# Attention loop of a four-layer graph network: the target one-hot on GpSimd, targets loaded first, the MLP's first layer beside its second

## What is computed

```python
wk = relu(edge_features @ k_w1 + k_b1) @ k_w2 + k_b2      # an MLP of two layers
wv = relu(edge_features @ v_w1 + v_b1) @ v_w2 + v_b2
k  = wk * sum_s sh[:, s] * (x_dst @ Cqk[:, s, :])          # s over 9
v  = wv * sum_s sh[:, s] * (x_dst @ Cv[:, s, :])
attn  = sum over each head of q[edge_src] * k              # 8 heads of 16
amax  = segment_max(attn, edge_src)
ex    = exp(attn - amax[edge_src])
denom = segment_sum(ex, edge_src)
upd   = segment_sum(v * ex / denom[edge_src], edge_src)
```

## Time and profile before

| what | us |
|---|---|
| median of three runs | 5155.87 |
| lowest, highest | 5151.41, 5162.44 |
| the profiled execution, its own time | 5154.97 |
| its span, first to last instruction | 5153.2 |
| mean granted TensorE clock, of 1 | 0.854 |

### The profile page before, as it was taken

The page is one execution under the profiler, slowest core; times in us unless marked ns, Lnnn a source line. Parts: engine busy times, 40 slices in busy tenths (PEclk is TensorE's granted clock), DMA queues, the critical chain, the costliest instruction groups (busy, mean ns, idle before and its releaser), DMA issues. The chain is left out here.

```text
span 5153.2 us, 91855 instructions
## 1 busy us (share of the span) xinstructions
PE 4427.7 (86%) x21874; PEld 3147.8 (61%) x21874; DVE 4161.0 (81%) x9462; ACT 2259.1 (44%) x4914; POOL 2409.1 (47%) x2660
## 2 busy tenths in 40 slices
PE   1788877879999999999999999999998677777777
PEld 0222343557777777777777777777777566666665
DVE  5999956479999999999999999999996455555554
ACT  0777740045555555555555555555553100000000
POOL 1000000045555555555555555555552377777774
PEclk7999978789999999999999999999998555555555
DMA  2121116377777777777777777777773244444442
GB/s 56 75 92 83 75 50 262 122 170 175 176 176 175 177 176 175 174 176 175 176 174 174 175 175 176 174 175 176 174 175 78 63 102 103 103 103 102 103 102 64
DMA packets 576584, 719.34 MB, mean 140 GB/s; under 512 B 204519, under 2 KB 338727, under 8 KB 572583
## 3 DMA queue, kind: packets, MB, share of 16 engines
q1 hardware_dynamic: 517910, 634.65, 49.1%
q0 software_dynamic: 52288, 81.11, 7.3%
q10 hardware_dynamic: 6288, 2.48, 0.2%
HBM read 663.58 MB, written 54.36 MB: 139 GB/s over the span
## 5 line engine op out<-in xcount | busy, mean ns | idle before, releaser
L1328 POOL DMA_INDIRECT attn_rows<-x_twice,attn_idx x808 | 988.4, 1223 | 237.6 <-issue 198.3
L1684 POOL DMA_INDIRECT msg_rows<-a_rows,msg_idx x808 | 778.9, 964 | 370.3 <-issue 241.2
L1271 ACT CAST attn_z_hi<-attn_z 128x512 fp32r<-128x512 f32 x1010 | 621.9, 620 | 184.9 <-DVE attn_z L1526 155.1
L1526 DVE TENSOR_TENSOR attn_z<-attn_xt,attn_sh 128x512 f32<-128x512 f32 x1010 | 679.0, 689 | 27.1 <-ACT attn_xt L1259 6.1
L1347 POOL TENSOR_TENSOR acc_den<-acc_den,attn_sums 128x256 f32 x808 | 582.0, 720 | 188.7 <-POOL acc_den L1347 151.9
L1722 PE MATMUL msg_at_dst<-msg_bwin,msg_pick 128*128 128x64 f32 x1616 | 397.7, 428 | 270.8 <-DVE msg_pick L1748 193.3
L1722 PEld LDWEIGHTS msg_at_dst<-msg_bwin,msg_pick 128*128 128x128 f32 x1616 | 359.9, 328 | 351.1 <-DVE msg_pick L1748 227.9
L1532 DVE TENSOR_TENSOR attn_z_lo<-attn_z,attn_z_hi 128x512 fp32r<-128x512 f32 x808 | 551.2, 682 | 0.8 <-ACT attn_z_hi L1271 0.7
L1662 ACT ACTIVATE msg_msg<-msg_pre 128x256 f32<-128x256 f32 x202 | 84.1, 417 | 941.5 <-DVE msg_pre L1763 937.1
L1349 POOL MEMSET acc_den<- 128x6656 f32 x1 | 5.6, 5646 | 978.6 <-POOLq L90 978.6
L538 PE MATMUL count_bank<-count_key_hot,count_lo_hot 128*128 128x400 bf16 x1395 | 328.7, 346 | 137.8 <-DVE count_key_hot L496 134.5
(11 more groups left out here) (293 smaller groups left out, 10927.0 us busy)
## 6 DMA issues: line engine op xcount, KB each, us to landing
attn_sh<-in_edge_sh SPq DMA_DIRECT2D x404, 640.0 KB
attn_dst<-dst_scaled SPq DMA_DIRECT2D x202, 256.0 KB
attn_qwin<-q_rows SPq DMA_DIRECT2D x808, 64.0 KB
attn_mask<-dst_step SPq DMA_DIRECT2D x202, 256.0 KB, 3.4
msg_dst<-dst_scaled SPq DMA_DIRECT2D x202, 256.0 KB, 3.2
counts<-chunk SPq DMA_DIRECT2D x15, 3100.0 KB, 9.7
chunk_late<-counts SPq DMA_DIRECT2D x15, 3100.0 KB, 10.4
attn_feat<-in_edge_feat SPq DMA_DIRECT2D x404, 64.0 KB
```

The lines of the kernel that those rows point to most:

```text
L1271: nc.scalar.copy(z_hi[p][:, c, :], z[:, c % 2, :]).then_inc(high_sb, 1)
L1328: pool.indirect_dma_start(rows[p][:, t, :], None, dram["x_twice"], bass.IndirectOffsetOnAxis(ap=idx[p][:, t:t + 1], axis=0)).then_inc(rows ...
L1526: dve.tensor_tensor(z[:, c % 2, :], xt[p][:], sh[p][:, c, :], ALU.mult).then_inc(z_ready, 1)
L1684: pool.indirect_dma_start(rows[p][:, t, :], None, dram["a_rows"], bass.IndirectOffsetOnAxis(ap=idx[p][:, t:t + 1], axis=0)).then_inc(rows_ ...
```

## The change

- `make_onehot` leaves VectorE. GpSimd makes it now, for group g instead of g-1: after the backward scan of g (`topped`) it runs four `tensor_scalar` comparisons of 128 columns, each with one column of targets as scalar. Their four target columns are copied to a small tile `local[p]` by ScalarE first. `onehot` gets two buffers. GpSimd's loop is then add, make_onehot, gather.
- `pick` gets two buffers, and VectorE's `make_pick(g+2)` moves from behind `maxima(g)` to ahead of it, into the place of `make_onehot`.
- SyncE loads `dst` first of a group's transfers.
- The MLP's first layer leaves `prepare` and stands directly ahead of the second layer, behind the k product. Its second half goes to the bank `b_attn` instead of `b_v`. ScalarE's third rounding `high(g+1, 2)` goes ahead of the relus.

```diff
@@ scalar body @@
                 if next:
+                    high(g + 1, q, 2)
                     hidden(g + 1, q)
-                    high(g + 1, q, 2)
...
+                if front:
+                    if not (is_first(g, 0) or is_first(g, 1)):
+                        act.wait_ge(onehot_ready, g - 1)
+                    nc.scalar.copy(local[p][:], sb["dst_local"][:, bass.ds(TG * g, TG)]).then_inc(local_sb, 1)
@@ gpsimd @@
+            def make_onehot(g, p):
+
+                pool.wait_ge(topped, g + 1)
+                pool.wait_ge(local_sb, g + 1)
+                if not (is_first(g, 0) or is_first(g, 1)):
+                    pool.wait_ge(sum_ps, g - 1)
+                pool.sem_inc(pool_go, 1)
+                for t in range(TG):
+                    op = pool.tensor_scalar(onehot[p][:, t, :], sb["iota_row"][:],
+                                            local[p][:, t:t + 1], None, ALU.is_equal)
+                op.then_inc(onehot_ready, 1)
...
             with pool.Fori(0, G // 2 - 3) as n:
                 add(2 * n + 1, 1)
+                make_onehot(2 * n + 3, 1)
                 gather(2 * n + 6, n + 3, 0, False)
                 add(2 * n + 2, 0)
+                make_onehot(2 * n + 4, 0)
                 gather(2 * n + 7, n + 3, 1, False)
@@ sync load @@
+                if not first:
+                    sp.wait_ge(pick_ready, g - 1)
+                sp.dma_start(dst[p][:], dram["dst_scaled"][bass.ds(g * GE, GE)].partition_broadcast(P)
+                             ).then_inc(dst_in[p], 16)
                 if not first:
                     sp.wait_ge(hid_ps, g - 1)
...
-                    sp.wait_ge(pick_ready, g - 1)
-                sp.dma_start(dst[p][:], dram["dst_scaled"][bass.ds(g * GE, GE)].partition_broadcast(P)
-                             ).then_inc(dst_in[p], 16)
-                if not first:
                     sp.wait_ge(q_ps, g - 1)
@@ tensor @@
                 mm.then_inc(xt_ps, 1)
+
+            def hidden(g, n, p):
                 pe.wait_ge(feat_in[p], 32 * (n + 1))
                 if not is_first(g, 0):
                     pe.wait_ge(hid_sb, 2 * g)
                 if not (is_first(g, 0) or is_first(g, 1)):
-                    pe.wait_ge(vw_ready, g - 1)
+                    pe.wait_ge(shifted, 2 * (g - 1))
                 nc.tensor.matmul(b_hid_vt[:, 0:GE // 2], sb["L2_w1"][0:D, :], feat[p][0:D, :], start=True, stop=True)
-                nc.tensor.matmul(b_v[:, 0:GE // 2], sb["L2_w1"][D:P, :], feat[p][D:P, :], start=True,
+                nc.tensor.matmul(b_attn[:, 0:GE // 2], sb["L2_w1"][D:P, :], feat[p][D:P, :], start=True,
                                  stop=True).then_inc(hid_ps, 1)
...
                     split_product(b_k, "L2_Cqk", g, p, True).then_inc(k_ps, 1)
+                if next:
+                    hidden(*after(g, n, p))
+                if front:
                     pe.wait_ge(hid_sb, 2 * (g + 1))
...
-                    if next:
-                        pe.wait_ge(hid_sb, 2 * (g + 2))
                     split_product(b_v, "L2_Cv", g, p, False).then_inc(v_ps, 1)
...
+                    if next:
+                        pe.wait_ge(hid_sb, 2 * (g + 2) - 1)
                     for t in range(TG):
                         nc.tensor.transpose(b_hid_vt[:, t * P:(t + 1) * P], vx[:, t * P:(t + 1) * P], sb["ident"][:])
...
                     pe.wait_ge(u_ready, g + 1)
+                    if next:
+                        pe.wait_ge(hid_sb, 2 * (g + 2))
                     nc.tensor.matmul(b_attn[:], sb["head_sum"][:], u[:], start=True, stop=True).then_inc(attn_ps, 1)
@@ vector @@
             def make_pick(g, n, p):
                 dve.wait_ge(dst_in[p], 16 * (n + 1))
-                if not is_first(g, 0):
-                    dve.wait_ge(q_ps, g)
+                if not (is_first(g, 0) or is_first(g, 1)):
+                    dve.wait_ge(q_ps, g - 1)
...
                     dve.tensor_tensor(vw[p][:], b_v[:], wv[:], ALU.mult).then_inc(vw_ready, 1)
-                if back:
-                    make_onehot(g - 1)
+                if has_two(g):
+                    make_pick(*in_two(g, n, p))
                 if front:
                     maxima(g, n, p)
-                if has_two(g):
-                    make_pick(*in_two(g, n, p))
```

More of the change, by code:

```diff
@@ L1167, in attention_loop @@
                                 "kw_ready", "u_ready", "vw_ready", "dve_set"))
-        xt_sb, hid_sb, w_sb, ex_sb, vt_sb, sum_sb, high_sb = (
-            ph.sem(n) for n in ("xt_sb", "hid_sb", "w_sb", "ex_sb", "vt_sb", "sum_sb", "high_sb"))
+        xt_sb, hid_sb, w_sb, ex_sb, vt_sb, sum_sb, high_sb, local_sb = (
+            ph.sem(n) for n in ("xt_sb", "hid_sb", "w_sb", "ex_sb", "vt_sb", "sum_sb", "high_sb", "local_sb"))
         vx_ready = ph.sem("vx_ready")
@@ L1190, in attention_loop @@
         wv = ph.sb("wv", [P, GE])
-        pick = ph.sb("pick", [P, TG, P])
-        onehot = ph.sb("onehot", [P, TG, P])
+        pick = [ph.sb(f"pick{p}", [P, TG, P]) for p in two]
+        onehot = [ph.sb(f"onehot{p}", [P, TG, P]) for p in two]
         u = ph.sb("u", [P, GE])
@@ L1200, in attention_loop @@
         zero = ph.sb("zero", [P, 1])
+        local = [ph.sb(f"local{p}", [P, TG]) for p in two]
         vt = ph.sb("vt", [P, TG, HD])
@@ L1263, in hidden @@
                 act.wait_ge(hid_ps, g + 1)
-                for half, bank in enumerate((b_hid_vt, b_v)):
+                for half, bank in enumerate((b_hid_vt, b_attn)):
                     nc.scalar.activation(hid[p][:, half * (GE // 2):(half + 1) * (GE // 2)], bank[:, 0:GE // 2], ACT.Relu,
@@ L1355, in _ @@
             gather(3, 1, 1, False)
+            make_onehot(0, 0)
             gather(4, 2, 0, False)
+            make_onehot(1, 1)
             add(0, 0)
+            make_onehot(2, 0)
             gather(5, 2, 1, False)
@@ L1360, in _ @@
                 add(2 * n + 1, 1)
+                make_onehot(2 * n + 3, 1)
                 gather(2 * n + 6, n + 3, 0, False)
                 add(2 * n + 2, 0)
+                make_onehot(2 * n + 4, 0)
                 gather(2 * n + 7, n + 3, 1, False)
             add(G - 5, 1)
-            for g in range(G - 4, G):
-                add(g, g % 2)
+            for g in range(G - 3, G):
+                make_onehot(g, g % 2)
+                add(g - 1, (g - 1) % 2)
+            add(G - 1, 1)
         @block.sync
@@ L1424, in pick_q @@
                 for t in range(TG):
-                    mm = nc.tensor.matmul(b_q[:, t * P:(t + 1) * P], qwin[p][:, t, :], pick[:, t, :],
+                    mm = nc.tensor.matmul(b_q[:, t * P:(t + 1) * P], qwin[p][:, t, :], pick[p][:, t, :],
                                           start=True, stop=True)
@@ L1483, in body @@
                     for t in range(TG):
-                        nc.tensor.matmul(b_wk_sum[:, t * P:(t + 1) * P], vt[:, t, :], onehot[:, t, :],
+                        nc.tensor.matmul(b_wk_sum[:, t * P:(t + 1) * P], vt[:, t, :], onehot[q][:, t, :],
                                          start=True, stop=True)
                     for t in range(TG):
-                        mm = nc.tensor.matmul(b_wv_den[:, t * P:(t + 1) * P], et[:, t, :], onehot[:, t, :],
+                        mm = nc.tensor.matmul(b_wv_den[:, t * P:(t + 1) * P], et[:, t, :], onehot[q][:, t, :],
                                               start=True, stop=True)
@@ L1492, in first @@
                 prepare(g, n, p)
+                hidden(g, n, p)
                 pick_q(g, n, p)
@@ L1510, in make_pick @@
                 dve.wait_ge(dst_in[p], 16 * (n + 1))
-                if not is_first(g, 0):
-                    dve.wait_ge(q_ps, g)
-                dve.tensor_tensor(pick[:], dst[p][:].rearrange("p (t e) -> p t e", t=TG),
+                if not (is_first(g, 0) or is_first(g, 1)):
+                    dve.wait_ge(q_ps, g - 1)
+                dve.tensor_tensor(pick[p][:], dst[p][:].rearrange("p (t e) -> p t e", t=TG),
                                   sb["node_of_part"][:, bass.ds(TG * g, TG)].unsqueeze(2).to_broadcast([P, TG, P]),
@@ L1573, in maxima @@
                                          in1=zero[:], op0=ALU.subtract, op1=ALU.min).then_inc(shifted, 1)
-            def make_onehot(g):
-                if not is_first(g, 0):
-                    dve.wait_ge(sum_ps, g)
-                dve.tensor_tensor(onehot[:], sb["iota_row"][:].unsqueeze(1).to_broadcast([P, TG, P]),
-                                  sb["dst_local"][:, bass.ds(TG * g, TG)].unsqueeze(2).to_broadcast([P, TG, P]),
-                                  ALU.is_equal).then_inc(onehot_ready, 1)
             def body(g, n, p, next, front, back):
```

## The result

The changed kernel takes 5138.2 us (median of 13 runs, 5129.7 to 5146.6) where the kernel before takes 5155.9 us in the same rounds. The ratio is 0.9967, with a 95% interval of 0.9957 to 0.9976: 18 us faster, where 80 were forecast. The sign was right and the size was not. The profiled execution took 5145.29 us, with a span of 5143.6.

A forecast was written before the change was run, and what follows sets the result against it. VectorE was taken as the bound at 14.20 us a group; -0.60 - 0.05 + 0.20 = -0.45, less 0.05 given back to TensorE, is -0.40, over 201 groups -80 us: 5075 us, forecast range 5040 to 5120 us.

The forecast's parts named there:

- What bounds the kernel now: Attention loop: VectorE runs without a gap and is the bound, 14.20 us a group; TensorE waits for it once a group.
- The pick in the one-hot's place: VectorE: the pick leaves its slot behind the maxima for the hole before the forward scan, -0.60 and -0.05 us a group.
- The wait of `vx` for exp: VectorE: `vx`, moved 0.60 us earlier, would wait for ScalarE's exp, +0.13 to 0.18 us, overlapping with the contention term.
- Four comparisons of 0.34 us: GpSimd: one comparison takes 0.34 us (bounds 0.19 and 0.64), four take 1.4 us (0.8 to 2.6); GpSimd has room.
- Contention on VectorE, +0.20 us: Two comparisons on GpSimd lengthen VectorE's z products; with the wait of `vx` for exp, +0.20 us a group together.
- the slow rival: Comparisons block both z products and `vx` in full, 1.02 us: +0.37 us a group, 5229 us; chance 0.12.
- The rows they fetch are used about one group later: GpSimd's gathers move behind the comparisons, to 2408.8 until 2414.6; their rows are used about one group later, no cost counted.
- a rival of chance 0.08: The gain is given back: late z products and fourth low, or late rows from gathers 2.5 us later; 5135 to 5156 us.
- the signs of being wrong: Comparison over 0.7 us, z products or `vx` 0.9 us, waits for `attn_rows` or `attn_dst`, fourth rounding releasing VectorE, TensorE never waiting.
- the 0.05 given back to TensorE: In the sum: 13.75 us a group is just above TensorE's floor, so 0.05 is given back, leaving -0.40 us.
- TensorE's floor of 13.7, later 13.5 us: TensorE's own list without its wait for `u` needs 13.7 us a group, about 13.5 with the MLP's move; the next limit.
- The targets first on SyncE: SyncE: `dst` is issued first, `sh` moves back by one issue and 256 KB; 7.1 us idle a group hide it, cost 0.

The follow-up runs named there:

- the last run: Changed kernel with the one-hot on ScalarE, transposes of rows ahead of the sums on TensorE and gathers one group further ahead: ratio 0.9753, 5029.5 us against 5156.8.

## Why the prediction was wrong, step by step

**What bounds the kernel now: right.** VectorE was the bound; the MLP's move alone, which touches only TensorE and ScalarE, gave nothing.

**The pick in the one-hot's place, -0.60 and -0.05 us: the step that failed.** It is the largest error of the sum. The hole was there and the pick fits it. But the prediction took everything behind the scan to move up by the whole slot. z also needs `xt`, and that comes from TensorE, which between the sum over heads and the transposes has the pick of query rows and the sums to do: 3.64 us, whatever VectorE does. The timeline of TensorE in the changed kernel:

```profile
2403.96 1.12 PE L1508 MATMUL attn_b_attn<-attn_u,head_sum 128*128 128x512 f32 x2 [0.36 <-DVE attn_u L1620]
...
2407.60 0.60 PE L1434 MATMUL attn_b_xt<-ident,attn_rows 128*128 128x128 f32 x4
```

With no comparison on GpSimd the whole change to VectorE's list gave 14.20 - 13.85 = 0.35 us a group, not 0.65; 0.25 of the other 0.30 came back when the transposes were moved. The prediction had seen this kind of tie for exp and missed it for `xt`. The wait of `vx` for exp, which it did count, came twice in the whole loop: z was late already.

**Four comparisons of 0.34 us: mis-priced, at little cost.** The price was taken from an affine select; the real one is nearly twice that, and more in company:

```profile
L1362 POOL TENSOR_SCALAR attn_onehot<-iota_row,attn_local x808: 590/620/1634, 1085.1 to 3935.8; 128x128 f32<-128x128 f32 x162
```

```profile
3934.05 2.53 POOL L1362 TENSOR_SCALAR attn_onehot<-iota_row,attn_local 128x128 f32<-128x128 f32 x4 [5.90 <-DVE attn_top L1597]
```

Beside a VectorE that mostly waits, at the loop's end, four take 2.53 us (0.63 each, the upper end of the bounds). In the loop they take 3.8 us. In the group shown above the first two take 0.62 and 0.60 us, and the two that run beside z and `vx`, which read both inputs from SBUF, take 1.37 and 1.32:

```profile
L1362 POOL TENSOR_SCALAR attn_onehot<-iota_row,attn_local x1: 602/602/602, 2408.7 to 2408.7; 128x128 f32<-128x128 f32 x1
L1362 POOL TENSOR_SCALAR attn_onehot<-iota_row,attn_local x1: 1374/1374/1374, 2409.3 to 2409.3; 128x128 f32<-128x128 f32 x1
```

The prediction said that GpSimd is the bound from 1.0 us each. With adds that grew as well, from 3.92 us (2402.14 to 2406.06) to 4.86 (2403.24 to 2408.10), its list was full at 0.96. The bound it was not: no other engine waited for it.

**Contention on VectorE, +0.20 us: right in kind, somewhat too large.** It measured 13.98 - 13.85 = 0.13 us, and by the table 0.14 to 0.15. `vx` grew from 0.72 to 0.78 us (it is 0.69 with no comparison beside it), and z hardly. The rule of the Trainium skill quoted in the prediction ("SBUF — State Buffer", "Who interferes with whom") is borne out in its pair of instructions; here it was mostly GpSimd that stood still, for 3.85 - 2.53 = 1.3 us of the comparisons shown. So the slow rival (VectorE blocked for 1.02 us) did not come.

**"The rows they fetch are used about one group later": the second failed step, a term put at nothing.** The gathers start 5.2 us later, not 2.5, and now behind `sh`, the largest transfer. Rows waited for in 51 of 141 groups cost 0.17 us a group. The price of the comparisons is not to blame: with one comparison of 0.62 us the gathers start 6.4 us behind `u`, earlier than the 7.0 us of the prediction's own sum (2408.8 - 2401.83), and the table shows the same loss. The prediction had named late rows within a rival of chance 0.08, whose 5135 to 5156 us are where the result fell; but its sum rests on 0.55 us of late products of VectorE, which did not come; late rows gave 0.17 us, and the chain over `xt` the rest. Of the signs of being wrong two came, the wait for `attn_rows` and comparisons of over 0.7 us (1.37 in the row above).

The terms by the runs: -0.35 where the prediction had -0.65 (pick and one-hot off VectorE, held by `xt`), +0.13 for +0.20 (comparisons beside VectorE's products), +0.17 for 0 (late rows), and 0 for the 0.05 given back to TensorE: -0.05 us for -0.40. These are differences between the runs' own groups, so that they end at 14.15 us proves nothing; the check is the run with one comparison, where 13.85 + 0.17 = 14.02 stands against 14.01 measured.

**TensorE's floor of 13.7, later 13.5 us: not met.** Its wait for `u` stayed at 51.3 / 141 = 0.36 us a group where under 0.2 was forecast. It is 0.36 us with the MLP's move alone too (51.4 / 141), and still 42.8 / 147 = 0.29 us in the last run, at 13.60 us a group. The wait was no measure of how far VectorE's list could shrink.

**The targets first on SyncE: no cost, as forecast.** VectorE waits for `dst` once in the whole loop. No run takes this move out, so what the old order would have cost is not shown.

## What to carry to other kernels

When time is taken out of the bounding engine, ask of every instruction behind the cut what else it waits for and how far ahead that is: here 0.35 of 0.65 us was all that could be gained, because one input came from a chain that did not move. Before a step is moved onto an engine that is half idle, look at what is queued behind it there, above all transfers, and how soon their data is needed. An engine without idle time need not be the bound: ask which other engine waits for it, and whether its instructions are drawn out by a neighbour. An order that loses 4% can win 1% once its input is early enough, so moves that fail are worth repeating after the wait they exposed is gone.

## What the runs showed that I had not expected

A comparison with a per-partition scalar on 128x128 f32 takes GpSimd 0.62 us in the median, where an affine select of the same shape takes 0.33 and an add of 128x256 with two inputs 0.64. The same one-hot as four absolute differences and one relu takes ScalarE 1.28 + 0.63 = 1.9 us:

```profile
2400.76 1.28 ACT L1278 ACTIVATE attn_dist<-iota_row,attn_local 128x128 f32<-128x128 f32 x4
2402.07 0.63 ACT L1284 ACTIVATE attn_onehot<-attn_dist 128x512 f32<-128x512 f32 x1
```

Rows land late and do so at a distance that no row of before shows. In the run with the one-hot on ScalarE and the earlier transposes, the last gather of a group and the transposes that wait for it are

```profile
2411.91 0.95 POOL L1345 DMA_INDIRECT attn_rows<-x_twice,attn_idx  x1 [0.31 <-issue]
```

```profile
2420.95 0.66 PE L1428 MATMUL attn_b_xt<-ident,attn_rows 128*128 128x128 f32 x4 [0.50 <-DMA attn_rows<-x_twice,attn_idx]
```

2420.95 - 2412.86 = 8.1 us behind the last gather's issue, with `sh` and the other transfers of a group under way on the same DMA engines.

Open is how near GpSimd's list is to being the bound. With eight comparisons it is one, with four it is full but nobody waits for it, and no run here takes the earlier transposes together with gathers further ahead and four comparisons on GpSimd, where it could be the next limit.
